# Mask and row maxima of the second scores in one product of 115 rows, the maxima moved by memory

## What is computed

```
q, k, v = heads(layernorm(x) @ Wq + bq), heads(ctx @ Wk + bk), heads(ctx @ Wv + bv)    # 16 heads of 16
scores  = q k^T / 4;  scores = where(mask, -1e15, scores);  attn = softmax(scores)
x = x + tanh(g_xattn) * ((attn v) @ Wo + bo)
y = layernorm(x);  w = renormalised top 3 of softmax(tanh(mean(y) @ W1 + b1) @ W2 + b2)   # 8 zones
x = x + tanh(g_ffn) * (y + sum over the zones z of w[z] * gelu(y @ Wa[z]) @ Wb[z])
```

## Time and profile before

| | |
|---|---|
| profiled execution | 368.46 us |
| its span | 366.7 us |
| TensorE matmul busy | 321.9 us, 88% |
| VectorE / ScalarE / GpSimd busy | 202.9 / 194.7 / 159.4 us |
| first phase | until 230.3 us (last `lo_part`) |
| second phase | first product at 233.07 us |

### The profile page before, as it was taken

One profiled execution on the slowest core, in us unless ns is written; L12 is line 12 of the kernel. 1 busy time (PEld: TensorE's weight loads), 2 busy tenths in 40 slices (PEclk: granted clock), 3 DMA queues, 4 the chain that ended last, 5 costly groups with the idle time before them and its releaser, 6 DMA issues.

```text
span 366.7 us, 10035 instructions
## 1 busy us (share of the span) xinstructions
PE 321.9 (88%) x3732; PEld 269.1 (73%) x3732; DVE 202.9 (55%) x607; ACT 194.7 (53%) x398; POOL 159.4 (43%) x219
## 2 busy tenths in 40 slices
PE   1766899799799998999999878579889999999996
PEld 1543576576576776767777556479889999999996
DVE  4335457367267477575675944266555555455452
ACT  3244366565565765665667567344446545554442
POOL 4863866458559569576598868200100000000000
PEclk9958699999899999999999999699999999999999
DMA  8956847748547658556376414010101011011000
GB/s 176 271 142 179 213 124 193 158 129 212 134 132 188 163 133 238 165 154 184 83 198 168 146 54 118 17 39 2 45 22 39 6 37 39 4 39 35 7 14 13
DMA packets 32927, 40.47 MB, mean 110 GB/s; under 512 B 9993, under 2 KB 26689, under 8 KB 32881
## 3 DMA queue, kind: packets, MB, share of 16 engines
q1 hardware_dynamic: 26176, 22.07, 23.4%
q0 software_dynamic: 4784, 16.98, 16.4%
q10 hardware_dynamic: 1920, 0.79, 0.9%
HBM read 33.09 MB, written 6.74 MB: 109 GB/s over the span
## 4 chain that ended last, share of the span: by engine, by line
PE 65%; POOL 9%; DMA 7%; DVE 7%; issue 5%; ACT 4%; DVEq 1%; SPq 0%; ACTq 0%; POOLq 0%
PE bank L1182 15%; PE bank L1201 15%; PE bank L1031 6%; PE bank L1039 5%; PE bank L979 4%; POOL wa L447 4%; PE bank L989 4%; DMA stage<-in_L_ffn_Wa 3%; PE bank L1013 3%; PE bank L999 3%; PE bank L993 3%; PE bank L1056 2%; DMA stage<-in_L_ffn_Wb 2%; DVE bank L741 2%; POOL stage L442 2%
## 5 line engine op out<-in xcount | busy, mean ns | idle before, releaser
L741 DVE CUSTOM_DVE_ANT_0 bank<-bank,maskb 112x375 f32<-112x375 f32 x128 | 67.7, 568 | 37.5 <-PE bank L979 37.2
L1182 PE MATMUL bank<-ctxT,wqkvo 128*128 128x112 f16 x960 | 61.4, 216 | 10.5 <-DVE qbd L909 10.5
L1182 PEld LDWEIGHTS bank<-ctxT,wqkvo 128*128 128x128 f16 x960 | 59.0, 100 | 12.1 <-issue 11.8
L1201 PE MATMUL bank<-wb,stage 128*112 x576 | 66.8, 273 | 0.0
L1201 PEld LDWEIGHTS bank<-wb,stage 128*112 128x112 f16 x576 | 62.3, 130 | 0.2
L529 ACT ACTIVATE pT<-bank 125x448 f32<-125x448 f32 x96 | 48.9, 540 | 19.5 <-PE bank L999 19.3
L706 ACT ACTIVATE kst<-bank 128x448 f32<-128x448 f32 x48 | 25.7, 535 | 57.4 <-PE bank L1182 57.4
L447 POOL TENSOR_TENSOR wa<-stage,wa 128x512 f16<-128x512 f32 x32 | 36.7, 1158 | 23.8 <-ACT wa L628 23.6
L908 DVE COPY wqkvo<-wa 128x3072 f16 x24 | 23.2, 966 | 43.1 <-PE bank L1182 38.3
L442 POOL TENSOR_SCALAR stage<-stage 128x512 f32<-128x512 f32 x64 | 39.3, 625 | 15.5 <-DMA stage<-in_L_ffn_Wa 9.2
L979 PE MATMUL bank<-kst,qbd 128*112 128x375 f16 x128 | 36.6, 349 | 10.6 <-DVE peaks L741 7.0
(11 more groups left out here) (115 smaller groups left out, 467.4 us busy)
## 6 DMA issues: line engine op xcount, KB each, us to landing
stage<-in_L_ffn_Wa POOLq DMA_DIRECT2D x16, 512.0 KB, 5.1
stage<-in_L_ffn_Wb POOLq DMA_DIRECT2D x16, 512.0 KB, 4.9
kst<-k_scr SPq DMA_DIRECT2D x64, 93.8 KB, 3.9
k_scr<-k_hl SPq DMA_DIRECT2D x16, 187.5 KB
ctx_s<-in_ctx SPq DMA_DIRECT2D x8, 336.0 KB
qbd<-q_scr SPq DMA_DIRECT2D x32, 56.0 KB, 3.2
xa<-in_x SPq DMA_DIRECT2D x8, 112.0 KB, 2.3
q_scr<-q_hl SPq DMA_DIRECT2D x32, 28.0 KB
```

The lines of the kernel that those rows point to most:

```text
L741: v.tensor_tensor_reduce(out=bank[0:SQ, e, 0:SK], in0=bank[0:SQ, e, 0:SK], in1=maskb[:, b % 2, 0:SK], scale=-1.0, scalar=3.0e38, op0=ALU.a ...
L1182: ins = T.matmul(o, first(ws, t, f), x2b[:, b % 2, (xs * DT + t) * SQ:(xs * DT + t + 1) * SQ], start=(t == 0 and xs == 0 and ws == 0), sto ...
L1201: ins = T.matmul(o, hT[:, u % 2, hs * FT * SQ + f * SQ:hs * FT * SQ + (f + 1) * SQ], wb[:, bass.ds(e * (4 * CHUNK) + ws * (2 * CHUNK) + f ...
```

## The change

- The mask's identity and the selector of the maxima become one moving operand `rq` of 115 rows: 112 rows of the identity, four times side by side, and 3 rows with the three parts of the maxima of four heads. The mask operand `maskb` gets three rows of ones. The four products with `pick` go away; a tile has one product of 115 rows and two of keys and queries.
- Rows 112 to 114 of `rq` (two buffers, by slot parity) are filled from memory: `write_max` stores `ms` (12 rows) to `m_scr`, `move_max` reads three rows back for each slot. Both stand in SyncE's queue, whose order is changed around them.
- First scores of batch n: pairs 0 to 7 all in iteration b, two pairs in each of slots 0 to 3. So the read half for pairs 0 to 3 is used from slot 0.
- MX1 and MX0 are transposed between the second and third tile of slots 0 and 2. K0 and K1 are projected before Q. `mask_bias` moves from slot 0 to slot 3 of the iteration before. `split_max` of pairs 4 to 7 moves to slot 3.
- The maxima are capped (FLOOR), and a 126th row of the last values tile holds the sum of all values scaled by a tiny number, which decides the output of a fully masked row: `cx_copy` also sums its rows on both engines (accum_out), the last values and `pv` products have 126 rows, `v_copy` has a scale. In the start, GpSimd fills `rq` in place of `pick` and `ms` (one copy and two selects for two memsets and three selects), and VectorE sets rows of `maskb` and `pT` to one.

```
     n, m, o = b + 1, b + 2, b - 1
     every = (
-        (("V0", n), ("XT", m), ("V1", n), ("MX1", b), ("CX0", m), ("CX1", m)),
-        (("Q", m), ("OT", o), ("K0", m), ("K1", m), ("X2T", b - 2)),
-        (("ON", o),),
-        (("MX0", n), ("OP", o)),
+        (("MX1", b), ("V0", n), ("XT", m), ("V1", n), ("CX0", m), ("CX1", m)),
+        (("K0", m), ("K1", m), ("Q", m), ("OT", o), ("X2T", b - 2)),
+        (("MX0", n), ("ON", o)),
+        (("OP", o),),
...
+        m_scr = nc.dram_tensor("m_scr", [B, 2, 12, 2, SQ], BF16).ap()
...
+            def write_max(b, h):
+                if there(b):
+                    sp.wait_ge(s["ms_done"], 2 * b + h + 1)
+                    sp.dma_start(m_scr[b, h, :, :, :], ms[:, :, :]).then_inc(s["m_written"], 16)
+
+            def move_max(b, g):
+
+                if there(b):
+                    sp.wait_ge(s["m_written"], 16 * (2 * b + g // 2 + 1))
+                    need(sp, s["pe_st"], tile(b, g, 0) - KC)
+                    sp.dma_start(rq[SQ:KQ, g % 2, :].rearrange("c (j q) -> c j q", j=4),
+                                 m_scr[b, g // 2, :, g % 2, :].rearrange("(c j) q -> c j q", j=4)).then_inc(rq_in[g % 2], 16)
+
             def load_xr(b):
                 if there(b):
                     need(sp, s["r_written"], b * 16 - 16)
...
             sp.dma_start(wqkvo[:, 2, :, :], view_w(Wv)).then_inc(s["wv_loaded"], 16)
             for b in range(-2, B):
                 n, m, o = b + 1, b + 2, b - 1
+                move_max(b, 1)
                 read_q(n, 1)
                 read_k(n, 1)
+                write_max(b, 1)
                 load_xr(o)
                 load_mask(m)
                 load_x(m + 1)
-
                 load_ctx(m + 1)
-                write_q(m)
-                store_r(b - 2)
-
+                move_max(b, 2)
                 write_k(m, 0)
                 write_k(m, 1)
-                store_x2(b - 2)
+                move_max(b, 3)
+                write_q(m)
+                write_max(n, 0)
                 if b == B - 1:
                     store_index(0)
                     sp.wait_ge(s["xt_done"], B)
...
                     load_x2(0)
                     load_x2(1)
+                read_k(m, 0)
+                move_max(n, 0)
                 read_q(m, 0)
-                read_k(m, 0)
+                store_r(b - 2)
+                store_x2(b - 2)
             load_xr(B - 1)
             store_r(B - 2)
             sp.wait_ge(s["pe_st"], tile(B, 0, 0))
...
                     full(act, name)
-                    c, n = ((0, 2), (2, 1))[half_]
+                    c, n, rows_ = ((0, 2, CK), (2, 1, CK + 1))[half_]
                     at = (b % 2) * (KC * NH * VC) + c * (NH * VC)
-                    a.activation(bass.AP(vp, at, [[2 * KC * NH * VC, CK], [VC, n * NH], [1, HD]]),
-                                 spare_bank(name)[0:CK, 0:n * D].rearrange("p (h i) -> p h i", i=HD), ACT.Copy).then_inc(s["v_done"], 1)
+                    if b == 0:
+                        act.wait_ge(s["ones_ready"], 2)
+                    a.activation(bass.AP(vp, at, [[2 * KC * NH * VC, rows_], [VC, n * NH], [1, HD]]),
+                                 spare_bank(name)[0:rows_, 0:n * D].rearrange("p (h i) -> p h i", i=HD), ACT.Copy,
+                                 scale=vsc[0:rows_, :]).then_inc(s["v_done"], 1)
...
                     name = ("MX%d" % h, b)
                     full(act, name)
-                    need(act, s["pe_st"], tile(b - 1, 2 * h + 2, 0))
-                    a.activation(ms[0:12, 2 * h:2 * h + 2, :].rearrange("r c q -> r (c q)"),
+                    need(act, s["m_written"], 16 * (2 * b + h))
+                    a.activation(ms[0:12, :, :].rearrange("r c q -> r (c q)"),
                                  spare_bank(name).bitcast(BF16)[0:12, 0:2 * SQ], ACT.Copy).then_inc(s["ms_done"], 1)
             def cx_copy(b):
                 if there(b):
                     name = ("CX0", b)
                     full(act, name)
-                    a.activation(ctxT[:, 0, :], spare_bank(name)[:, 0:SK], ACT.Copy).then_inc(s["cx0_done"], 1)
...
                 exp_tile(b, 0, 1)
+                max_copy(b, 1)
                 o_copy(o)
                 exp_tile(b, 0, 2)
-                mask_bias(n)
                 v_copy(n, 0)
                 xt_copy(m)
                 v_copy(n, 1)
-                max_copy(b, 1)
                 cx_copy(m)
                 for k in parts_at(b, 0):
                     w_hi(k)
...
                     a.activation(bq_c[:, :], bq_c[:, :], ACT.Copy, scale=HD ** -0.5).then_inc(s["wq_scaled"], 1)
                     act.wait_ge(s["wq_scaled"], 2)
                     act.wait_ge(s["bk_loaded"], 16)
-                q_hi(m)
                 k_hi(m, 0)
                 k_hi(m, 1)
+                q_hi(m)
                 for k in parts_at(b, 1):
                     w_hi(k)
                 if b == B - 1:
...
                 exp_tile(b, 2, 0)
                 exp_tile(b, 2, 1)
+                max_copy(n, 0)
                 exp_tile(b, 2, 2)
                 x2_hi(b - 2)
                 ot_copy(o)
...
                 exp_tile(b, 3, 1)
                 exp_tile(b, 3, 2)
-                max_copy(n, 0)
+                mask_bias(m)
                 for k in parts_at(b, 3):
                     w_hi(k)
                 normed(m + 1)
...
                     if p == 0:
                         dve.wait_ge(s["mask_ready"], b + 1)
+                    if p % HP == 0 and b > 0:
+                        full(dve, ("MX%d" % (p // HP), b - 1))
                     for e in range(2):
                         dve.wait_ge(s["pe_s1"], s1_no(b, p, e) + 1)
-                        v.tensor_tensor_reduce(out=bank[0:SQ, e, 0:SK], in0=bank[0:SQ, e, 0:SK], in1=maskb[:, b % 2, 0:SK],
-                                               scale=-1.0, scalar=3.0e38, op0=ALU.add, op1=ALU.min,
-                                               accum_out=peaks[:, p // 2, TOP[b % 2], p % 2 * 2 + e:p % 2 * 2 + e + 1]).then_inc(s["dve_max"], 1)
+                        v.tensor_tensor_reduce(out=bank[0:SQ, e, 0:SK], in0=bank[0:SQ, e, 0:SK], in1=maskb[0:SQ, b % 2, 0:SK],
+                                               scale=-1.0, scalar=FLOOR, op0=ALU.add, op1=ALU.min,
+                                               accum_out=peaks[:, p // 2, TOP, p % 2 * 2 + e:p % 2 * 2 + e + 1]).then_inc(s["dve_max"], 1)
...
                     full(dve, name)
-                    v.tensor_copy(ctxT[:, 1, :], spare_bank(name)[:, 0:SK]).then_inc(s["cx1_done"], 1)
+                    if b == 0:
+                        dve.wait_ge(s["ident_ready"], 1)
+                    src = spare_bank(name)[:, 0:SK]
+                    v.tensor_tensor_reduce(out=ctxT[:, 1, 0:SK], in0=src, in1=bass.AP(half, 0, [[1, 128], [0, SK]]), scale=-2.0, scalar=0.0, op0=ALU.mult, op1=ALU.add,
+                                           accum_out=ctxT[:, 1, SK:SK + 1]).then_inc(s["cx1_done"], 1)
             def k_lo(b, t):
...
                     full(dve, name)
+                    dve.wait_ge(s["parts_done"], min(2 * b + 5, 2 * B))
                     src = spare_bank(name)[0:SQ, :].rearrange("q (g j i) -> q g j i", j=4, i=32)
                     st.link(v.reciprocal(peaks[:, :, NEG, :].rearrange("q g (j o) -> q g j o", o=1), src[:, :, :, HD:HD + 1]))
...
-                row_max(b, 7)
-                split_max(b, 1)
+                row_max(n, 0)
+                row_max(n, 1)
                 cx_copy(m)
                 if b == B - 1:
                     route_logits(0)
-                row_max(n, 0)
-                row_max(n, 1)
-                if b == -2:
-                    dve.wait_ge(s["wq_scaled"], 2)
-                q_lo(m)
-                o_rows(o)
-                if b == -2:
-                    dve.wait_ge(s["bk_loaded"], 16)
-                k_lo(m, 0)
-                result(b - 2)
-                k_lo(m, 1)
-                if b == B - 1:
-                    route_top(0)
-
                 row_max(n, 2)
                 row_max(n, 3)
                 split_max(n, 0)
+                if b == -2:
+                    dve.wait_ge(s["wq_scaled"], 2)
+                    dve.wait_ge(s["bk_loaded"], 16)
+                k_lo(m, 0)
+                k_lo(m, 1)
+                q_lo(m)
+                o_rows(o)
+                result(b - 2)
+                if b == B - 1:
+                    route_top(0)
+
+                row_max(n, 4)
+                row_max(n, 5)
                 x2_lo(b - 2)
                 ln1_stats(m + 1)
-                row_max(n, 4)
-                row_max(n, 5)
+                row_max(n, 6)
+                row_max(n, 7)
+                split_max(n, 1)
                 residual(o)
                 if b == -1:
                     dve.wait_ge(s["const_loaded"], 80)
...
                     need(pe, s["act_exp"], t - len(ST_BANKS) + 1)
                     o = bank[:, ST_BANKS[t % len(ST_BANKS)], 0:QUAD]
```

(44 more changed lines are left out.)

70 lines of the change are left out of this document (38 added, 32 removed).

## The result

The changed kernel takes 391.55 us (median of 4 runs, 389.22 to 394.58) against 368.47 for the kernel before: ratio 1.067 with a 95% interval of 1.062 to 1.072. The prediction was 367.5 and its range ended at 376, so it was wrong, and on the side to which I had given 0.26. The profiled execution took 394.58 us, with a span of 392.5.

A forecast was written before the change was run, and what follows sets the result against it. GpSimd's loop beside a nearly full TensorE was taken as the bound. Start +6.6, five iterations -4.5, the next +0.7 and end -3.6 gave -0.8 us: 367.5 us forecast against 368.09, range 357 to 376.

The forecast's parts named there:

- the side to which I had given 0.26: The chance forecast for a change that is slower; faster by over 1% had 0.36, within 1% had 0.38.
- What bounds the kernel before: Step on the old kernel: TensorE nearly full, 23.10 of 24.58 us per iteration, with a second loop through GpSimd beside it.
- GpSimd's loop: From the mark via K1 in slot 1, ScalarE's w_hi, GpSimd's ten us, normed and exponential; w_hi to next mark 11.95 us.
- B: Rival: TensorE's pace decides if loads and GpSimd keep up, five iterations of 22.2 us, 357 us in all; chance 0.36.
- the tie: From K1's end to the mark, the moves' chain takes 13.4 us and GpSimd's loop 13.45, so the moves' wait is hidden.
- the mark: Start of the third tile of slot 0, from which iterations are counted.
- The new moves: Step timing writes, moves and reads from K1's end: TensorE waits some 2 us at slot 0, mark at 13.4 us.
- Rival C: The wait at the start of slot 0 lowers the clock, 1.4 us in six of the iterations, 376 us; chance 0.17.
- Rival D: Moves land late behind large transfers, 5 to 6 us instead of 3.2; iterations grow 2 to 2.5, 381 us; chance 0.06.
- 23.7: Forecast us per iteration under GpSimd's loop, 0.9 less than 24.58.
- Start, end, other edits: Steps outside the steady iterations: first mark 6.6 us later, end 3.6 us earlier, other edits at most about 0.2 us.
- The sixth iteration: The one from 169.23, without a norm1 before: it now waits for the reads at 23.5 us, +0.7.

The follow-up runs named there:

- g_direct: Kernel before with the 115-row product, maxima moved by one DMA into rq ahead of the queries' reads, norm1 right behind add_bo: 355.63 us, ratio 0.963.
- e_const: Changed kernel with constant zero rows for the maxima, which are neither stored, moved nor subtracted: 378.44 us, ratio 1.033 to the kernel before.
- h_fill: Changed kernel with 16 products without use ahead of the maxima's wait at slot 0's first tile: 382.31 us, ratio 1.040 to the kernel before.
- h_after: Changed kernel without edit, run again on the same chip as h_fill: median 393.78 us over six runs (386.45 to 396.95).
- e_actq: Changed kernel with the maxima's store issued from ScalarE's queue right behind their copy, not SyncE's: 385.45 us, ratio 1.038 to the kernel before.
- e_pick: Changed kernel's order of work, but maxima subtracted by four selector products per tile, without store or move: 383.26 us, ratio 1.048 to the kernel before.

## Why the prediction was wrong

**What bounds the kernel before** was right. GpSimd's loop behind `norm1` held it: one moved line gives 2.8%, and the product by itself, in the old order, 0.6%. A time like B's 357 came only with that line moved (g_direct, 355.63). GpSimd's side of the tie held in the changed kernel as well: `norm1` ended at 159.33, 12.3 us after the end of K1, and the mark stood 1.1 us behind it in the kernel before, which makes 13.4 where I had 13.45.

**The failed step is "The new moves".** I count again from the end of K1, 147.08 in the iteration shown. The low half of the keys was ready at 1.3 (forecast 1.3), slot 3's move landed at 5.4 (5 to 6.2), the store of the maxima was issued at 5.25 (until 5.4), the reads of k until 7.6 (7.3), and TensorE was done with slot 3 at 9.4 (9.5). So far each term held. Then came what I had mis-sized, the landing of the store above all:
- I took the store as landed by about 7.3, two microseconds after its issue, without a row for it. It landed 4.3 us after, at 9.55. As SyncE's queue runs in order, the reads of q stood behind that wait too.
- The move was issued from there and landed 3.15 later, at 12.7, where I had 10 to 11.5. Its issue held SyncE for 0.75 us, not 0.4.
- The queries came at 13.4, not 11.6. Even without maxima they come at 13.8 (e_const), since their read waits for the landing of their own write, 5.7 us. I had counted the four issues of that write and no landing, although the k writes' 3.7 us stood in the same sentence.
- From the first scores to the mark it took 2.3 us where I had 1.8, at the lower clock. The mark is at 15.7 instead of 13.4.

**The tie broke.** I had 13.4 for this chain and 13.45 for GpSimd's, and called the wait hidden. With two chains so close, any term too short comes out whole.

**The clock.** Rival C, at 0.17, had the mechanism, and h_fill shows it: with the store as late as ever, a TensorE that does not idle is 5 to 11 us faster. Rival D, at 0.06, had the lateness, but not its place: in the chain the moves landed 2.8 to 3.9 us after their issue and not 5 to 6, and what came late was the store ahead of them. I priced each alone, on top of a free wait. The two prices together, 23.7 + 2.2 + 1.4 = 27.3 us per iteration, come near the 27.6 that the first six took on average; as neither was worked out for what happened, that fit is partly luck. They were not independent: the lateness makes the idle time, and the idle time lowers the clock.
The Trainium skill (TensorE: Matmul & The Clock Gate, "What's actually happening") has throttled as the default state, released by activity. The trace agrees: the granted clock is 0.51 behind the wait of 3.43 us, and 1.00 throughout the iterations of h_fill, whose TensorE is kept busy there.

**Start, end, other edits.** The first mark was forecast 6.6 us late and came 9.0 late, 6.9 in h_after; e_const has 6.8, so the start belongs to the order. The two last iterations and the second phase gave back 1.1 of the 3.6 forecast. The sixth iteration lost 5.0, not 0.7. The product of 115 rows cost nothing beyond the one of 112 (0.193 us both), as assumed.

**What stays open.** Which part of the new order costs its 3.3%: the wait points at the shift of the first scores, but no run undid that alone. How much of the store's 4.3 us is its place behind the writes of q was not separated: in e_actq queue and issue time changed together. Nor was g_direct tried without its moves, which would tell what they still cost there.

## What to carry to other kernels

A value that goes through memory costs two landings and two places in a queue. Count each landing from its row, the write's as well as the read's, and give a store without a row the nearest write's, not a guess. When operands are needed one slot earlier, redo the whole round trip for every operand, not only for the one that the change is about. And before counting a gain on the busiest engine, see whether its last wait belongs to another loop: here one moved line on GpSimd gave 2.8%, and 384 products taken off TensorE gave 0.6% without it.

## What the runs showed of the hardware

- A store of 5.2 KB from 12 partitions landed 4.3 us after its issue behind four writes of 28 KB, and 2.9 and 5.1 us after in other iterations of the same run. The write of q landed 2.8 to 5.6 us after its last issue over the iterations of e_pick, and 3.4 to 6.2 over those of e_const.
- A DMA of 2.6 KB into three partitions held SyncE's queue for 0.75 us, more than one of 28 KB (0.6).
- The changed kernel's time varied by 2.7% over six runs on one chip, in step with its mean granted clock (0.929 to 0.901), and with the idle time filled by 1.4% (h_fill, six runs). Idle time alone does not make the spread: e_const, whose TensorE idles 20.9 us for the queries, varied by 0.5% over four runs.
